# One stage in place of three in the third layer of a graph network kernel

## The chip, the cores and the metric

The kernel runs on one core of one Trainium2 chip. A core has five engines with instruction streams of their own: TensorE (PE, matrix products, with its weight loads shown as PEld), VectorE (DVE), ScalarE (ACT), GpSimd (POOL) and SyncE (SP), and 16 DMA engines that move data between the core's memory and HBM. Each engine runs its stream strictly in order and waits on semaphores that others raise. The metric is the device time of one execution in microseconds (us), the median of several executions.

## The reference

Four graph layers stand behind each other; the third is the one concerned. It runs four steps over 5000 nodes with a state `h` of 128 numbers each and 80000 edges of four types:

```python
etypes = jnp.argmax(edge_feat, axis=1)
h = node_feat
for _ in range(N_STEPS):                                   # 4
    trans = jnp.einsum('nd,tod->tno', h, W_edge) + b_edge[:, None, :]
    msg = trans[etypes, src]
    a = jax.ops.segment_sum(msg, dst, num_segments=N)
    h = _gru_cell(a, h, W_ih, W_hh, b_ih, b_hh)

# _gru_cell(x, h): gi = x @ W_ih.T + b_ih, gh = h @ W_hh.T + b_hh, each split in r, z, n parts
#   r = sigmoid(ir + hr); z = sigmoid(iz + hz); n = tanh(inn + r * hn)
#   return (1 - z) * n + z * h
```

## The kernel before

The nodes are padded to 5120, which makes ten chunks of 512 (`CHUNKS`, `CHUNK`). The state `hT` is kept turned, features on the 128 partitions and nodes along the free dimension. All numbers are 32-bit floats; PSUM has eight banks, each of 128 x 512.

The program is a row of blocks. Inside a block each engine has its own stream, and a block ends for all engines together (line 82 in the trace). Semaphores used by a block are cleared by SP in a later block; `clear_block` is an empty block for that, at the end of a loop body. Most dense stages use the helper `pairs`, which runs chunks two at a time (`V = 2`) in a hardware loop, so that chunk `c` uses buffers and banks `u = c % 2` and one chunk is worked on while the other is read out.

Each of the four steps of the third layer (the loop over `L2_STEPS`) runs four stages:

- `projected_rows` ("l2_rows"): DVE copies a chunk of `hT` to a staging tile `xs` (L775), PE multiplies its four groups of 128 nodes with the 128 x 512 matrix of all four edge types (L799), DVE adds the bias into `rows` (L781) and SP stores 1 MB per chunk in the table `table_typed` (L816). Both PSUM sides are double: banks `4 * u + k`.
- `sum_pass` ("l2_sums"): POOL gathers one row of the table for each edge (L857), DVE builds selection matrices (L961), PE adds the rows up in PSUM (L979), ACT copies each finished bank of sums to `t1` (L944). Nodes lie on partitions there.
- `from_rows` ("l2_messages"): DVE copies a chunk of `t1` to a staging tile (L1498), PE turns it with four transposes (L1567), DVE copies the turned chunk back to `t1` (L1541).
- `gru` ("l2_gru"): for each chunk PE makes six products of 512 columns into four banks (`4 * u` to `4 * u + 3`, L1633 to L1636), ACT bends two of them with a sigmoid (L1644, L1645), DVE applies the reset gate (L1656, L1659), ACT takes the tanh (L1649), DVE updates the state in three operations (L1663, L1665, L1667).

What sets the order on PE in `gru` is `pairs`: the products of both chunks of a pair stand behind each other, and they wait only for banks that were read out two chunks ago:

```python
def project(c, u, i):
    at_least(pe, g_gated, c + 1 - V)
    at_least(pe, g_read, c + 1 - V)
```

Of the kernel before, what the change touches and what calls it, by code (L numbers as in the profile page):

```python
# [67 lines left out]
def program(nc, io, out):  # L68
    ctx = ExitStack()
    with ctx:  # L70
        def sb(name, shape, dt=F32, where=ctx):
            return where.enter_context(nc.sbuf_tensor(name, shape, dt))

        def sems(*names):
            return [ctx.enter_context(nc.semaphore(n)) for n in names]
# [4 lines left out]
        @contextmanager  # L80
        def block(name, *used):
            with nc.Block(name) as b:  # L82
                cleared = [s for s in spent if s not in used]
                assert len(cleared) == len(spent), name
                spent.clear()

                @b.sync
                def _(sp):
                    for s in cleared:
                        sp.sem_clear(s)  # L90
                yield b
            spent.extend(used)

        def clear_block(name):
            with block(name):
                pass
# [4 lines left out]
        table_typed = nc.dram_tensor("table_typed", [NP, 4 * D], F32)  # L101
# [8 lines left out]
        ident = sb("ident", [P, P])  # L110
# [4 lines left out]
        wt = sb("wt", [P, NW, P])  # L115
# [11 lines left out]
        gate_bias = sb("gate_bias", [P, 2, 2])  # L127
# [5 lines left out]
        bedge_rows = sb("bedge_rows", [P, 4 * D])  # L133
# [26 lines left out]
        def wcol(name, k=0):  # L160
            return vec[:, VEC[name] + k:VEC[name] + k + 1]
# [4 lines left out]
        with ExitStack() as tmp:  # L166
# [395 lines left out]
        ROWS = LOOPS * GROUP * 16  # L562

        TILE_COUNTS = [len(range(r, TILE_REGIONS, REGIONS)) * GROUP * 16 for r in range(REGIONS)]
# [13 lines left out]
        V = 2  # L578
        def pairs(eng, *stages, ahead=None):


            turns_of = CHUNKS // V

            def run(i, parts):
                for stage in parts:
                    for u in range(V):
                        stage(i * V + u, u, i)

            def turn(i):
                if ahead is not None and not (isinstance(i, int) and i + 1 == turns_of):  # L590
                    run(i + 1, [ahead])
                run(i, stages)
            if ahead is not None:
                run(0, [ahead])
            turn(0)
            with eng.Fori(1, turns_of - (ahead is not None)) as i:
                turn(i)
            if ahead is not None:
                turn(turns_of - 1)
# [103 lines left out]
        r_stored = sems(*(f"rows_stored{u}" for u in range(V)))  # L703
# [917 lines left out]
        def gru(name, msg, h, w_ih, w_hh, gates, b_in, b_hn):  # L1621

            with ExitStack() as tmp:
                gate = sb(f"{name}_gate", [P, V, 2, CHUNK], F32, tmp)
                new = sb(f"{name}_new", [P, V, CHUNK], F32, tmp)
                with block(name, g_product, g_gated, g_reset, g_new, g_read, g_step) as b:
# [26 lines left out]
                    def _(dve):  # L1653
# [13 lines left out]
                            dve.tensor_tensor(h[:, cols(c)], new[:, u, :], gate[:, u, 0, :], ALU.add).then_inc(g_step, 1)  # L1667
                        pairs(dve, reset, update)

        b_stats, b_root, b_applied, b_scale, b_done = sems("bn_step", "bn_rooted", "bn_applied", "bn_product", "bn_done")  # L1670

        def batch_norm(name, src, gain, shift, dst=None, residual=None, weight=None, bias=None):
# [63 lines left out]
        def add_state(name, src):  # L1736
            with block(name, a_added) as b:
                @b.vector
                def _(dve):
                    dve.tensor_tensor(resT[:], resT[:], src[:], ALU.add).then_inc(a_added, 1)  # L1740
# [55 lines left out]
        def parts_of(w, first, count):  # L1796
            return [w[:, first + k, :] for k in range(count)]
# [27 lines left out]
        with block("l2_index", l_typed) as b:  # L1825
            @b.sync
            def _(sp):
# [3 lines left out]
                               (w3[:, 6:8, :], io["L3_gnn_W2"].rearrange("(k p) f -> p k f", p=P))):  # L1831
                    sp.dma_start(to, of).then_inc(l_typed, 16)
                sp.wait_ge(l_typed, 16 * 7)
        with nc.Fori(0, L2_STEPS) as it:
            projected_rows("l2_rows", hT, wt[:, WEDGE:WEDGE + 4, :].rearrange("p a b -> p (a b)"), 4 * D, table_typed, bias=bedge_rows[:])
            sum_pass("l2_sums", table_typed.ap().rearrange("n (t f) -> (n t) f", f=D),
                     [GAT_ITERS * ROWS + n + it * n for n in TILE_COUNTS], t1)
            from_rows("l2_messages", t1, rows_in=t1)
            gru("l2_gru", t1, hT, parts_of(wt, GGIH, 3), parts_of(wt, GGHH, 3), gate_bias[:, 1, :], wcol("2_b_ih", 2), wcol("2_b_hh", 2))
            clear_block("l2_end")  # L1840
        add_state("l2_residual", hT)


# [29 lines left out]
```

## Time and profile before

| | us |
|---|---|
| median of 3 runs | 12100.61 |
| lowest and highest | 12093.36, 12107.19 |
| the profiled execution | 12019.95 |
| its span, first to last instruction | 12018.1 |
| PE busy, share of the span | 6550.1 (55%) |
| POOL busy, share of the span | 6209.6 (52%) |
| DVE busy, share of the span | 4612.7 (38%) |
| ACT busy, share of the span | 2251.5 (19%) |

The busy shares are means over many stages with different limits, so they say little of one stage. The third layer's steps run from 6498 to 10673 us of the span. The profiled execution was 80.7 us shorter than the median of the unprofiled ones, of which 1.9 us lie around the span. TensorE's granted clock is shown as a share of 2.4 GHz: 1.00 is 2.4 GHz, 0.50 is 1.2 GHz, and a value between is a mean over a stretch that had both.

### The profile page before, as it was taken

Reading aid. Unit: us, or ns where it says so; the run is one execution under the profiler, and the core shown is the slowest. Engines: PE = TensorE matmul, PEld = TensorE weight load, DVE = VectorE, ACT = ScalarE, POOL = GpSimd, SP = SyncE. Lnnn points to the kernel's source line nnn. Section 1 sums busy time; section 2 is a strip of 40 time slices with the busy share of each in tenths; the row PEclk is TensorE's granted clock in tenths of the full one; section 3 lists DMA queues with packets and bytes.
Section 4 is the critical chain, followed back from the end, with each engine's and each line's share of the span. In section 5 each row is a group of like instructions: output and inputs, shape, how many; then the busy total and the mean of one; then the engine's idle time right before and its main releaser. Section 6 shows DMA issues by size and latency. Waiting matters only on the chain. (4 is left out here: it accounts for less than half of the span.)

```text
span 12018.1 us, 148393 instructions
## 1 busy us (share of the span) xinstructions
PE 6550.1 (55%) x36272; PEld 5479.0 (46%) x36273; DVE 4612.7 (38%) x10118; ACT 2251.5 (19%) x4313; POOL 6209.6 (52%) x6365
## 2 busy tenths in 40 slices
PE   3666786566786665884335334433533443365555
PEld 3555665555765555853323223233323322244443
DVE  4444754444754444752113112211311221135555
ACT  1222552222542222641000000000000000011111
POOL 2666423666414665504663665466366456625553
PEclk6777898777897777996667666666766666677777
DMA  2444322444313443401111111211111121112221
GB/s 75 128 127 127 103 64 69 128 127 125 106 42 88 129 128 105 125 22 42 46 45 61 46 46 36 68 45 46 60 45 45 34 71 46 46 43 77 78 77 55
DMA packets 698434, 894.29 MB, mean 74 GB/s; under 512 B 148417, under 2 KB 443211, under 8 KB 698130
## 3 DMA queue, kind: packets, MB, share of 16 engines
q0 software_dynamic: 198368, 429.61, 13.6%
q1 hardware_dynamic: 498474, 461.96, 12.4%
q8 instruction: 51, 0.84, 0.0%
q14 instruction: 125, 1.02, 0.0%
q10 hardware_dynamic: 1416, 0.86, 0.0%
HBM read 698.72 MB, written 193.14 MB: 74 GB/s over the span
## 5 line engine op out<-in xcount | busy, mean ns | idle before, releaser
L857 POOL DMA_INDIRECT states<-table_typed,tile_idx x2512 | 2415.9, 962 | 1777.8 <-issue 721.2
L840 POOL DMA_INDIRECT states<-table_x,src_idx x2016 | 1980.1, 982 | 1862.7 <-POOLq L82 742.8
L979 PE MATMUL psum<-states,l_sums_select 128*128 x4480 | 905.5, 336 | 1729.7 <-issue 1696.3
L979 PEld LDWEIGHTS psum<-states,l_sums_select 128*128 128x128 f32 x4480 | 777.0, 244 | 1854.3 <-issue 1853.8
L961 DVE SCALAR_TENSOR_TENSOR l_sums_select<-dst_all,pair_start,iota_row 128x512 f32<-128x512 f32 x560 | 402.1, 749 | 2212.5 <-remote 1401.0
L1091 PE MATMUL psum<-ident,select 128*128 128x128 f32 x2016 | 418.3, 344 | 1199.3 <-DVE states L1059 723.4
L840 POOL DMA_INDIRECT l_pass_ring<-table_kv,src_idx x672 | 655.1, 975 | 658.9 <-DVE score L1312 286.3
L1068 DVE TENSOR_TENSOR states<-w,psum 128x512 f32<-128x512 f32 x504 | 345.2, 685 | 1544.0 <-ACT w L1048 969.0
L857 POOL DMA_INDIRECT states<-table_x,tile_idx x628 | 602.1, 959 | 626.2 <-POOLq L82 337.0
L979 PE MATMUL psum<-states,select 128*128 x2240 | 469.4, 348 | 808.8 <-issue 769.4
L944 ACT COPY t<-psum 128x512 f32<-128x512 f32 x50 | 29.3, 585 | 4534.1 <-PE psum L979 2586.3
L1091 PEld LDWEIGHTS psum<-ident,select 128*128 128x128 f32 x2016 | 297.9, 178 | 1263.5 <-DVE states L1059 567.3
L979 PEld LDWEIGHTS psum<-states,select 128*128 128x128 f32 x2240 | 404.7, 254 | 876.7 <-issue 876.0
L1144 POOL TENSOR_TENSOR w<-iota_row,dst_local 128x512 f32<-128x512 f32 x504 | 524.3, 1041 | 459.7 <-ACT select L1161 459.7
L1108 PE MATMUL psum<-t,l_scores_spread 128*128 x4032 | 675.2, 317 | 72.1 <-issue 71.6
L1105 PE MATMUL psum<-wt,l_scores_mixT 128*128 128x128 f32 x4032 | 713.5, 336 | 0.0
L1105 PEld LDWEIGHTS psum<-wt,l_scores_mixT 128*128 128x128 f32 x4032 | 672.1, 252 | 0.6 <-issue 0.2
L1108 PEld LDWEIGHTS psum<-t,l_scores_spread 128*128 128x128 f32 x4032 | 630.4, 233 | 75.8 <-issue 75.7
L961 DVE SCALAR_TENSOR_TENSOR select<-dst_all,pair_start,iota_row 128x512 f32<-128x512 f32 x280 | 200.2, 749 | 1035.7 <-remote 567.1
L1231 PE MATMUL psum<-l_values_msg,select 128*128 128x132 f32 x4032 | 549.5, 279 | 68.2 <-DVE l_values_msg L1171 68.2
L1048 ACT COPY w<-psum 128x512 f32<-128x512 f32 x504 | 300.5, 596 | 1355.7 <-remote 844.0
L1220 PE MATMUL psum<-wt,l_values_ring 128*128 128x128 f32 x4032 | 535.7, 277 | 15.4 <-DMA l_values_ring<-rows_dram 15.4
(357 smaller groups left out, 11997.4 us busy)
## 6 DMA issues: line engine op xcount, KB each, us to landing
states<-in_edge_attr_dram SPq DMA_DIRECT2D x2016, 64.0 KB
rows_dram<-l_scores_mixT SPq DMA_DIRECT2D x504, 256.0 KB
l_values_ring<-rows_dram SPq DMA_DIRECT2D x504, 256.0 KB
table_typed<-l_rows_rows SPq DMA_DIRECT2D x40, 1024.0 KB, 4.3
states<-table_typed,tile_idx POOLq DMA_INDIRECT x2512
states<-table_x,src_idx POOLq DMA_INDIRECT x2016
l_pass_ring<-table_kv,src_idx POOLq DMA_INDIRECT x672
table_x<-l_rows_rows SPq DMA_DIRECT2D x40, 256.0 KB, 2.3
```

Of the source, the lines that this page charges most:

```text
L840: pool.indirect_dma_start(out=ring[:, k % REGIONS, u, :], out_offset=None, in_=table, in_offset=at).then_inc(gathered[k % REGIONS], 16)
L857: pool.indirect_dma_start(out=ring[:, k % TILE_RING, u, :], out_offset=None, in_=table, in_offset=at).then_inc(gathered[k % REGIONS], 16)
L961: dve.scalar_tensor_tensor(out=picked(k), in0=dst_all[:, bass.ds(column, GROUP)].unsqueeze(2).broadcast_to([P, GROUP, P]), scalar=pair_sta ...
L979: ins = pe.matmul(to, picked(k)[:, u, :], rows, start=False, stop=True, skip_group_check=True)
L1048: act.copy(key[:, r % 2, :, :], keys(r)).then_inc(p_evacuated, 1)
L1068: dve.tensor_tensor(prod.rearrange("p (a b) f -> p a b f", a=2), key[:, r % 2, :, :].rearrange("p (a b) f -> p a b f", a=2), queries(r)[:, ...
L1091: pe.transpose(psum[:, 0, u * P:(u + 1) * P], select[:, r, u, :], ident[:])
L1105: pe.matmul(keys(r)[:, u, :], mixT[:, r, u, :], wt[:, WK, :], start=True, stop=True)
L1108: ins = pe.matmul(queries(r)[:, u // pair, u % pair, :], spread[:, r % 2, u, :], q, start=True, stop=True)
L1144: pool.tensor_tensor(away[:, r % 2, :, :], iota_row[:].unsqueeze(1).broadcast_to([P, GROUP, P]), dst_local[:, bass.ds(step_of(i, r), GROUP ...
L1220: ins = pe.matmul(values(r)[:, u, :], ring[:, r, u, :], wt[:, WV, :], start=True, stop=True)
L1231: ins = pe.matmul(sums(r, u), select[:, r, u, :], msg[:, r, u, :], start=True, stop=True)
```

## The change

`from_rows`, `gru` and the next step's `projected_rows` become one block, `gated_update`, written out over ten chunks. Ahead of the loop stands one `projected_rows` and a `clear_block`; the loop runs three steps of `sum_pass` and `gated_update`; a fourth `sum_pass` and a `gated_update` without projection follow it. The transposes read `t1` in place and the projection reads `hT` in place; ACT copies the turned sums to `msgT`. The working tiles lie in `states`, which is free between two sum passes. The four gate banks are now banks 1 to 4 for every chunk, bank 0 holds the turned sums, and banks 5 to 7 go round for the projection.

`waves` runs the stages of different chunks in one order: at each turn `t`, projection of chunk `t - 2`, gates of chunk `t - 1`, turning of chunk `t`.

```diff
+        def gated_update(name, msg, h, w_ih, w_hh, gates, b_in, b_hn, rhs=None, bias=None, table=None):
...
+            def waves(*stages):
+                for t in range(CHUNKS + len(stages) - 1):
+                    for lag in reversed(range(len(stages))):
+                        if 0 <= t - lag < CHUNKS:
+                            stages[lag](t - lag)
...
+                    def turn(c):
+                        at_least(pe, u_copied, c)
+                        for k in range(4):
+                            ins = pe.transpose(psum[:, 0, k * P:(k + 1) * P], msg[:, c * CHUNK + k * P:c * CHUNK + (k + 1) * P], ident[:])
+                        ins.then_inc(u_turned, 1)
+                    def gates_of(c):
+                        at_least(pe, u_gated, c)
+                        at_least(pe, u_read, c)
+                        pe.matmul(psum[:, 4, :], w_hh[2], h[:, at(c)], start=True, stop=True)
+                        for k in range(2):
+                            pe.matmul(psum[:, 1 + k, :], w_hh[k], h[:, at(c)], start=True, stop=False)
+                        pe.wait_ge(u_copied, c + 1)
+                        for k in range(2):
+                            pe.matmul(psum[:, 1 + k, :], w_ih[k], msgT[:, c % V, :], start=False, stop=True)
+                        pe.matmul(psum[:, 3, :], w_ih[2], msgT[:, c % V, :], start=True, stop=True).then_inc(u_product, 1)
+                    def next_rows(c):
+                        pe.wait_ge(u_step, 3 * c + 3)
+                        for k in range(4):
+                            at_least(pe, u_kept, 4 * c + k - 2)
+                            pe.matmul(psum[:, 5 + (4 * c + k) % 3, :], h[:, c * CHUNK + k * P:c * CHUNK + (k + 1) * P], rhs,
+                                      start=True, stop=True).then_inc(u_projected, 1)
+                    waves(*([turn, gates_of, next_rows] if project else [turn, gates_of]))
...
+                    def copy(c):
+                        act.wait_ge(u_turned, c + 1)
+                        at_least(act, u_product, c + 1 - V)
+                        act.copy(msgT[:, c % V, :], psum[:, 0, :]).then_inc(u_copied, 1)
+                    def bend(c):
+                        act.wait_ge(u_product, c + 1)
+                        at_least(act, u_step, 3 * (c + 1 - V))
+                        act.activation(gate[:, c % V, 0, :], psum[:, 1, :], ACT.Sigmoid, bias=gates[:, 0:1])
+                        act.activation(gate[:, c % V, 1, :], psum[:, 2, :], ACT.Sigmoid, bias=gates[:, 1:2]).then_inc(u_gated, 1)
+                        act.wait_ge(u_read, c + 1)
+                        act.activation(new[:, c % V, :], new[:, c % V, :], ACT.Tanh, bias=b_in).then_inc(u_new, 1)
+                    waves(copy, bend)
...
+                    for t in range(CHUNKS + 1):
+                        if project and t >= 1:
+                            keep(t - 1, 0)
+                            keep(t - 1, 1)
+                        if t < CHUNKS:
+                            reset(t)
+                        if project and t >= 1:
+                            keep(t - 1, 2)
+                            keep(t - 1, 3)
+                        if t < CHUNKS:
+                            update(t)
...
+                            sp.dma_start(table[at(c), :].rearrange("(b p) f -> p b f", p=P), rows[:, c % V, :, :]).then_inc(r_stored[c % V], 16)
...
-        with nc.Fori(0, L2_STEPS) as it:
-            projected_rows("l2_rows", hT, wt[:, WEDGE:WEDGE + 4, :].rearrange("p a b -> p (a b)"), 4 * D, table_typed, bias=bedge_rows[:])
-            sum_pass("l2_sums", table_typed.ap().rearrange("n (t f) -> (n t) f", f=D),
-                     [GAT_ITERS * ROWS + n + it * n for n in TILE_COUNTS], t1)
-            from_rows("l2_messages", t1, rows_in=t1)
-            gru("l2_gru", t1, hT, parts_of(wt, GGIH, 3), parts_of(wt, GGHH, 3), gate_bias[:, 1, :], wcol("2_b_ih", 2), wcol("2_b_hh", 2))
...
+        projected_rows("l2_rows", hT, by_type, 4 * D, table_typed, bias=bedge_rows[:])
+        clear_block("l2_start")
+        with nc.Fori(0, L2_STEPS - 1) as it:
+            sum_pass("l2_sums", typed_rows, [GAT_ITERS * ROWS + n + it * n for n in TILE_COUNTS], t1)
+            gated_update("l2_update", t1, hT, *l2_gates, rhs=by_type, bias=bedge_rows[:], table=table_typed)
             clear_block("l2_end")
+        sum_pass("l2_last_sums", typed_rows, [GAT_ITERS * ROWS + L2_STEPS * n for n in TILE_COUNTS], t1)
+        gated_update("l2_last_update", t1, hT, *l2_gates)
```

`reset`, `update` and `keep` on DVE are the operations of L1656, L1659, L1663, L1665, L1667 and L781 of the kernel before, on the new tiles. In the changed kernel their lines are L1748, L1751 (reset), L1755, L1757, L1759 (update) and L1744 (keep); on PE L1700 is `turn`, L1706 to L1712 `gates_of`, L1718 `next_rows`.

In the kernel before, PE's stream at the start of the gated update holds the products of a pair of chunks (`t1` is the turned sums, `hT` the state, `wt` the weights):

```order
L1633 MATMUL psum<-t1,wt 128x512
L1634 MATMUL psum<-hT,wt 128x512
L1633 MATMUL psum<-t1,wt 128x512
L1634 MATMUL psum<-hT,wt 128x512
L1635 MATMUL psum<-t1,wt 128x512
L1636 MATMUL psum<-hT,wt 128x512
L1633 MATMUL psum<-t1,wt 128x512
```

In the changed kernel PE's stream from the start of the fused block reads (`states` is `msgT` there, and L1718 with `wt,hT` the projection of the chunk whose gates stand ahead of it):

```order
L1700 MATMUL psum<-ident,t1 128x128 x4
L1706 MATMUL psum<-hT,wt 128x512
L1708 MATMUL psum<-hT,wt 128x512 x2
L1711 MATMUL psum<-states,wt 128x512 x2
L1712 MATMUL psum<-states,wt 128x512
L1700 MATMUL psum<-ident,t1 128x128 x4
L1718 MATMUL psum<-wt,hT 128x512 x4
L1706 MATMUL psum<-hT,wt 128x512
L1708 MATMUL psum<-hT,wt 128x512 x2
L1711 MATMUL psum<-states,wt 128x512 x2
L1712 MATMUL psum<-states,wt 128x512
```

Between the gates of one chunk (first L1706 to L1712) and the gates of the next now stand four transposes and the projection of the first chunk.

DVE's stream of the kernel before, at the start of the gated update, holds two resets and then two updates:

```order
L1656 SCALAR_TENSOR_TENSOR l2_gru_new<-psum,vec,l2_gru_gate 128x512
L1659 TENSOR_TENSOR l2_gru_new<-l2_gru_new,psum 128x512
L1656 SCALAR_TENSOR_TENSOR l2_gru_new<-psum,vec,l2_gru_gate 128x512
L1659 TENSOR_TENSOR l2_gru_new<-l2_gru_new,psum 128x512
L1663 TENSOR_TENSOR l2_gru_gate<-hT,l2_gru_new 128x512
L1665 TENSOR_TENSOR l2_gru_gate<-l2_gru_gate 128x512
L1667 TENSOR_TENSOR hT<-l2_gru_new,l2_gru_gate 128x512
```

In the changed kernel it goes, from the update of the first chunk on (all working tiles are in `states`):

```order
L1755 TENSOR_TENSOR states<-hT,states 128x512
L1757 TENSOR_TENSOR states<-states 128x512
L1759 TENSOR_TENSOR hT<-states 128x512
L1744 TENSOR_TENSOR states<-psum,bedge_rows 128x512 x2
L1748 SCALAR_TENSOR_TENSOR states<-psum,vec,states 128x512
L1751 TENSOR_TENSOR states<-states,psum 128x512
L1744 TENSOR_TENSOR states<-psum,bedge_rows 128x512 x2
L1755 TENSOR_TENSOR states<-hT,states 128x512
```

Two of the four bias additions of one chunk now stand ahead of the next chunk's reset, and two between its reset and its update.

## Rows read from the trace of the kernel before

**Rows 1.** The page's first line: the span.

```profile
span 12018.1 us, 148393 instructions
```

**Rows 2.** Busy time by stage: sum pass, messages, gated update, table rows.

```profile
core 0: us, PE busy (x) PEld busy (x) DVE busy (x) ACT busy (x) POOL busy (x), PEclk, DMA share, GB/s
6551.00:7469.30 918.30, 329.65 (x1584) 277.04 (x1582) 139.81 (x196) 8.33 (x13) 604.70 (x628) 0.61 0.17 45
7469.30:7484.60 15.30, 8.97 (x40) 7.13 (x40) 10.31 (x20) 0.00 (x0) 0.00 (x0) 0.60 0.00 0
7484.60:7545.90 61.30, 53.90 (x120) 23.51 (x120) 34.01 (x51) 20.58 (x31) 0.00 (x0) 0.95 0.00 0
7545.90:7594.10 48.20, 37.18 (x80) 15.41 (x80) 27.99 (x51) 0.00 (x0) 0.00 (x0) 0.95 0.50 188
```

**Rows 3.** Timeline, stage borders: start, us, engine, line, operation, [idle before <-releaser].

```profile
7468.69 0.58 ACT L944 COPY t<-psum 128x512 f32<-128x512 f32 x1 [18.41 <-PE psum L979]
...
7547.18 0.17 DVE L788 MEMSET t<- 128x128 f32 x1 [1.32 <-PEq L82]
...
7591.58 2.48 DVE L781 TENSOR_TENSOR l_rows_rows<-psum,bedge_rows 128x512 f32<-128x512 f32 x4 [0.29 <-DMA table_typed<-l_rows_rows]
...
7599.71 0.94 POOL L857 DMA_INDIRECT states<-table_typed,tile_idx  x1 [155.02 <-POOLq L82]
...
10595.26 0.58 ACT L944 COPY t<-psum 128x512 f32<-128x512 f32 x1 [23.17 <-PE psum L979]
...
10671.76 0.69 DVE L1667 TENSOR_TENSOR hT<-l_gru_new,l_gru_gate 128x512 f32 x1
```

**Rows 4.** Timeline, the last pair of chunks of a gated update.

```profile
7537.83 1.02 PE L1636 MATMUL psum<-hT,wt 128*128 x2
7538.97 0.69 ACT L1644 ACTIVATE l_gru_gate<-psum,gate_bias 128x512 f32<-128x512 f32 x1 [3.88 <-PE psum L1636]
7539.56 0.68 ACT L1645 ACTIVATE l_gru_gate<-psum,gate_bias 128x512 f32<-128x512 f32 x1
...
7540.27 0.75 DVE L1656 SCALAR_TENSOR_TENSOR l_gru_new<-psum,vec,l_gru_gate 128x512 f32<-128x512 f32 x1 [3.33 <-ACT l_gru_gate L1645]
7541.06 0.69 DVE L1659 TENSOR_TENSOR l_gru_new<-l_gru_new,psum 128x512 f32<-128x512 f32 x1
...
7541.78 0.72 ACT L1649 ACTIVATE l_gru_new<-l_gru_new,vec 128x512 f32<-128x512 f32 x1 [0.93 <-DVE l_gru_new L1659]
...
7543.72 0.68 DVE L1663 TENSOR_TENSOR l_gru_gate<-hT,l_gru_new 128x512 f32<-128x512 f32 x1
...
7545.16 0.69 DVE L1667 TENSOR_TENSOR hT<-l_gru_new,l_gru_gate 128x512 f32 x1
```

**Rows 5.** Timeline, two chunks of the table rows.

```profile
7565.08 4.87 DVE L781 TENSOR_TENSOR l_rows_rows<-psum,bedge_rows 128x512 f32<-128x512 f32 x8
7565.82 7.13 PE L799 MATMUL psum<-wt,select 128*128 128x512 f32 x16 [1.25 <-DVE l_rows_rows L781]
```

**Rows 6.** Timeline of PE: first matmuls behind a wait (three from the score pass).

```profile
312.65 1.09 PE L1091 MATMUL psum<-ident,select 128*128 128x128 f32 x4 [4.99 <-ACT l_scores_mixT L1040]
...
818.99 0.66 PE L1091 MATMUL psum<-ident,select 128*128 128x128 f32 x4 [2.59 <-ACT l_scores_mixT L1040]
...
1115.08 0.66 PE L1091 MATMUL psum<-ident,select 128*128 128x128 f32 x4 [2.52 <-ACT l_scores_mixT L1040]
...
7547.68 8.64 PE L799 MATMUL psum<-wt,select 128*128 128x512 f32 x16 [8.82 <-DVE select L775]
```

**Rows 7.** Busy time and granted clock (PEclk) behind three of these waits.

```profile
312.60:317.60 5.00, 4.95 (x23) 4.99 (x24) 2.84 (x5) 1.47 (x3) 3.78 (x5) 0.50 0.53 151
...
818.80:821.00 2.20, 2.02 (x13) 2.02 (x14) 1.37 (x3) 1.11 (x4) 1.59 (x3) 0.70 0.34 115
821.00:826.00 5.00, 5.00 (x37) 4.99 (x36) 1.46 (x3) 0.59 (x2) 3.78 (x5) 0.79 0.59 173
...
7547.60:7550.70 3.10, 3.02 (x4) 1.48 (x5) 0.35 (x2) 0.00 (x0) 0.00 (x0) 0.50 0.03 8
```

More of the change, by code:

```diff
@@ L1668, in _, with at, keep, reset @@
                         pairs(dve, reset, update)
+        u_turned, u_copied, u_product, u_gated, u_reset, u_read, u_new, u_step, u_projected, u_kept = sems(
+            "sums_turned", "sums_copied", "gate_products", "gates_made", "reset_applied", "gate_banks_read", "new_made", "state_step",
+            "next_projected", "next_kept")
+        def gated_update(name, msg, h, w_ih, w_hh, gates, b_in, b_hn, rhs=None, bias=None, table=None):
+            room = states[:, 0:V * (4 + 4 * 4) * CHUNK // 2]
+            msgT = room[:, 0:V * CHUNK].rearrange("p (u f) -> p u f", u=V)
+            gate = room[:, V * CHUNK:3 * V * CHUNK].rearrange("p (u k f) -> p u k f", u=V, k=2)
+            new = room[:, 3 * V * CHUNK:4 * V * CHUNK].rearrange("p (u f) -> p u f", u=V)
+            rows = room[:, 4 * V * CHUNK:4 * V * CHUNK + V * 4 * CHUNK].rearrange("p (u k f) -> p u k f", u=V, k=4)
+            project = rhs is not None
+            def at(c):
+                return slice(c * CHUNK, (c + 1) * CHUNK)
+            def waves(*stages):
[3 more added lines that the diff above has]
+                            stages[lag](t - lag)
+            with block(name, u_turned, u_copied, u_product, u_gated, u_reset, u_read, u_new, u_step, u_projected, u_kept, *r_stored) as b:
+                @b.tensor
+                def _(pe):
+                    def turn(c):
[20 more added lines that the diff above has]
+                    waves(*([turn, gates_of, next_rows] if project else [turn, gates_of]))
+                @b.scalar
+                def _(act):
+                    def copy(c):
[10 more added lines that the diff above has]
+                    waves(copy, bend)
+                @b.vector
+                def _(dve):
+                    def keep(c, k):
+                        dve.wait_ge(u_projected, 4 * c + k + 1)
+                        if c >= V:
+                            dve.wait_ge(r_stored[c % V], c // V * 16)
+                        dve.tensor_tensor(rows[:, c % V, k, :], psum[:, 5 + (4 * c + k) % 3, :], bias, ALU.add).then_inc(u_kept, 1)
+                    def reset(c):
+                        dve.wait_ge(u_gated, c + 1)
+                        dve.scalar_tensor_tensor(out=new[:, c % V, :], in0=psum[:, 4, :], scalar=b_hn, in1=gate[:, c % V, 0, :],
+                                                 op0=ALU.add, op1=ALU.mult).then_inc(u_reset, 1)
+                        dve.wait_ge(u_reset, c + 1)
+                        dve.tensor_tensor(new[:, c % V, :], new[:, c % V, :], psum[:, 3, :], ALU.add).then_inc(u_read, 1)
+                    def update(c):
+                        dve.wait_ge(u_new, c + 1)
+                        dve.tensor_tensor(gate[:, c % V, 0, :], h[:, at(c)], new[:, c % V, :], ALU.subtract).then_inc(u_step, 1)
+                        dve.wait_ge(u_step, 3 * c + 1)
+                        dve.tensor_tensor(gate[:, c % V, 0, :], gate[:, c % V, 0, :], gate[:, c % V, 1, :], ALU.mult).then_inc(u_step, 1)
+                        dve.wait_ge(u_step, 3 * c + 2)
+                        dve.tensor_tensor(h[:, at(c)], new[:, c % V, :], gate[:, c % V, 0, :], ALU.add).then_inc(u_step, 1)
+                    for t in range(CHUNKS + 1):
[9 more added lines that the diff above has]
+                            update(t)
+                if project:
+                    @b.sync
+                    def _(sp):
+                        for c in range(CHUNKS):
+                            sp.wait_ge(u_kept, 4 * c + 4)
+                            sp.dma_start(table[at(c), :].rearrange("(b p) f -> p b f", p=P), rows[:, c % V, :, :]).then_inc(r_stored[c % V], 16)
+                        for stored in r_stored:
+                            sp.wait_ge(stored, 16 * (CHUNKS // V))
@@ L1833, in _ @@
                 sp.wait_ge(l_typed, 16 * 7)
-        with nc.Fori(0, L2_STEPS) as it:
-            projected_rows("l2_rows", hT, wt[:, WEDGE:WEDGE + 4, :].rearrange("p a b -> p (a b)"), 4 * D, table_typed, bias=bedge_rows[:])
-            sum_pass("l2_sums", table_typed.ap().rearrange("n (t f) -> (n t) f", f=D),
-                     [GAT_ITERS * ROWS + n + it * n for n in TILE_COUNTS], t1)
-            from_rows("l2_messages", t1, rows_in=t1)
-            gru("l2_gru", t1, hT, parts_of(wt, GGIH, 3), parts_of(wt, GGHH, 3), gate_bias[:, 1, :], wcol("2_b_ih", 2), wcol("2_b_hh", 2))
+        by_type = wt[:, WEDGE:WEDGE + 4, :].rearrange("p a b -> p (a b)")
+        typed_rows = table_typed.ap().rearrange("n (t f) -> (n t) f", f=D)
+        l2_gates = (parts_of(wt, GGIH, 3), parts_of(wt, GGHH, 3), gate_bias[:, 1, :], wcol("2_b_ih", 2), wcol("2_b_hh", 2))
+        projected_rows("l2_rows", hT, by_type, 4 * D, table_typed, bias=bedge_rows[:])
[3 more added lines that the diff above has]
+            gated_update("l2_update", t1, hT, *l2_gates, rhs=by_type, bias=bedge_rows[:], table=table_typed)
             clear_block("l2_end")
+        sum_pass("l2_last_sums", typed_rows, [GAT_ITERS * ROWS + L2_STEPS * n for n in TILE_COUNTS], t1)
+        gated_update("l2_last_update", t1, hT, *l2_gates)
         add_state("l2_residual", hT)
```

## The prediction

> **What bounds the kernel now.** I read the span first [rows 1], then cut one step of the third layer into its stages by busy time [rows 2]. The sum pass takes 918.3 us and is not touched; the change can only act on what stands between the end of one sum pass and the first gather of the next. The three stages there are 15.3, 61.3 and 48.2 us long. The reader should see which engine fills each: in the gated update PE is busy 53.9 of 61.3 us, in the table rows 37.2 of 48.2 us, and the granted clock is 0.95 in both, so PE's work at 2.4 GHz is the bound there, while in the messages stage it is a round between DVE and PE at a mean clock of 0.60. Third, I take the exact borders from the timeline [rows 3]: the last copy of sums ends at 7469.27 (7468.69 + 0.58), the last bias addition of the table rows at 7594.06, the first gather starts at 7599.71. From sums to the last bias addition are **124.8 us**, three times over. The last step has no table rows behind it: 10595.84 to 10672.45, **76.6 us**. The first table rows stay as they are.
>
> **PE's work per chunk.** A 32-bit product of 512 columns is two records. Eight of the projection's take 7.13 us [rows 5]; less about 0.2 us by which the last record outlasts its turn that is 0.86 us a product at full clock, and the gate products have the same length (L1636, 1.02 us with that overlap) [rows 4]. Six gate products make 5.14 us, four projections 3.43 us, together 8.57 us. Four transposes take 1.09 us at the low clock and 0.66 with overlap at the full one, some 0.43 us of pitch [rows 6]. So the fused stage asks PE for 9.0 us a chunk. None of this is saved. What goes are DVE's copies: L1498 and L1541, 20 operations in 10.3 us, with the messages stage of 15.3 us that they set [rows 2], and L775 in the table rows, where DVE is busy only 28.0 of 48.2 us, so that one costs little now.
>
> **What the change adds: a wait in PE's stream.** PE runs in order, and the order is gates of chunk c, turning of c+1, projection of c, gates of c+1. The projection waits for the finished state of chunk c, which needs the whole round trip through ACT and DVE; the gates of c+1, which need nothing of it, are queued behind that wait. Before, the gates of the next pair filled it. The length of the round trip, from rows 4: PE could start its next product at 7538.69 (7537.83 + 0.86). ACT's first sigmoid starts at 7538.97, the second ends at 7540.24, DVE's reset runs from 7540.27 and its second operation starts at 7541.06. Behind that, DVE now does two bias additions of the chunk before, 0.60 us apart each by (4.87 - 0.68) / 7 [rows 5], so the update can start at 7542.86; the tanh would be done at 7542.50, so the two additions, and not the tanh, come last, by 0.36 us. The update takes 2.13 us, from 7543.72 to 7545.85 in its row, so it ends at 7545.0, and PE starts 0.05 us later. That is **6.36 us** in which PE has 0.43 us of transposes. At full clock a chunk takes 8.57 + 6.36 = 14.93 us.
>
> ACT's new copy (0.58 us, as L944 [rows 3]) and the turning of the next chunk lie inside this wait; both are free as long as the wait is there. The table load that ACT does once at the sigmoid lies ahead of the first product. The stores (1 MB a chunk) have two chunks' time to land; before they made DVE wait only 0.29 us at the end [rows 3], where a chunk took 4.2 us. Behind the last bias addition the store and the block end take the same 5.6 us to the first gather as before.
>
> **The clock.** What does PE's clock do behind a wait of almost 6 us? Behind 4.99 us of waiting in the score pass it resumed at 1.2 GHz and stayed there for 5.0 us of work; behind 8.82 us, at the head of the table rows, for 3.1 us [rows 6, 7]. Half of such a stretch is lost: 2.5 and 1.55 us. I take 2.0 us a chunk, the middle, which gives **16.93 us**. The Trainium skill ("TensorE: Matmul & The Clock Gate", section "HAM oscillation — how this bites in real kernels") says that waits between bursts throttle PE again each time, so that every burst starts cold; rows 6 and 7 agree. By that rule alone the sum would be the same as with rows.
>
> **The sum, fused stage.** Block start 0.35 us, first chunk's turning and gates 7 us (5.6 at full clock, up to 1.5 more), nine further chunks 152.4 us, and at the end the round trip, projection at a partly low clock and last addition, 6.36 + 3.43 + 2.0 + 0.8 = 12.6 us: 172.3 us in place of 124.8. That is +47.5 us, three times: **+142.6**. Clear blocks: an empty block costs about 1 us (a border with one took 1.32 us in row L788 [rows 3], one without about 0.35); before one lay inside each 124.8 us, now it lies behind each fused stage and one ahead of the loop: +3 net.
>
> **The last update** has no projection, but its gate banks are no longer double: gates of c+1 wait until DVE has read chunk c's banks, 7541.75 + 0.05 less 7538.69, 3.11 us [rows 4]. At full clock a chunk takes 8.25 us, where two chunks of the gated update before took 61.3 / 5 = 12.3 us, 6.1 each. PE waits 2.7 us of it. Behind 2.59 us the clock fell just after PE had resumed (granted 0.70, then 0.79 over 7.2 us, 3.4 us at 1.2 GHz, 1.7 lost), behind 2.52 us the four transposes ran at the full rate, as their 0.66 us show [rows 6, 7]. Our wait is longer than both; I take 1.45 us a chunk, 9.7 us. 0.35 + 7 + 87.3 + 6.0 for the last round trip = 100.7 us in place of 76.6: **+24.1**. The Trainium skill ("Perfetto Trace Analysis", section "Matmuls") advises to let matmul groups go round through PSUM banks so that reading out one overlaps the next; the gate banks now do the opposite, and the trace agrees: with two sets a chunk took 6.1 us.
>
> All together 142.6 + 3 + 24.1 = **+170 us**. The profiled execution took 12019.95 us and would take 12190; against the median, 80.7 us higher, 12100.6 + 170 = **12270**.
>
> **The rivals.**
> - *The clock stays at 2.4 GHz.* Against it, rows 6 and 7; for it, only that 2.52 us did nothing. Fused stage 0.35 + 5.8 + 134.4 + 10.6 = 151.1, last 0.35 + 5.8 + 74.3 + 6 = 86.4: 79 + 3 + 10 = +92, 12192 us.
> - *The clock never rises.* A chunk takes 17.14 + 6.36 = 23.5 us, the fused stage 237, the last 138: +400, 12501 us. Against it: both long waits were followed by a rise after 3 to 5 us of work, and PE has 9 here.
> - *Faster: PE is not held up*, because the wait for the state is shorter than I read, or covered. It decides where the round trip falls under the 0.43 us of transposes. Then PE's 9.0 us a chunk is the period: 0.35 + 5.8 + 81 + 10.6 = 97.8 us, and 62 in the last: -81 + 3 - 14 = -92, 12008 us. The profile speaks against it: ACT's two sigmoids and DVE's five operations stand one behind the other in rows 4. The Trainium skill ("Perfetto Trace Analysis", section "Optimization Strategy") says that interleaving stages with different limits may help; that would be this case, and no row here supports it, since both long stages have the same limit, PE.
>
> **How the numbers follow.** Chances: forecast 0.84, full clock 0.08, low clock 0.03, faster 0.04, no change 0.01. Bounds of the forecast: low stretches of 3.1 to 5.0 us over some 30 bursts, -13 to +15; four stage starts, -6 to +6; the last update without a fall or with 1.7 us each, -13 to +2; code written out over ten chunks that has to be fetched, 0 to +15; spread of runs 7. That is about 12225 to 12315; I give 12225 to 12320. About 0.2% (24 us) is what a measurement of this kernel can tell from no change. Faster 0.04, same 0.01, slower 0.95.
>
> **What would show it.** In the changed profile, PE should wait about 5.9 us in each chunk of the fused stage ahead of L1718, released by DVE's L1759, with a granted clock well under 0.95 there; a chunk should take 16 to 18 us, and the sums should be 172 us ahead of the last bias addition. In the last update PE waits some 2.7 us for L1751. Sum passes stay at 918 us; if they move, the forecast is wrong for a reason that I haven't seen. It falls if PE waits for something else, or if L1744 holds up the update by more than 0.4 us.

## The result and the profile after

| | median us | lowest, highest | runs |
|---|---|---|---|
| before | 12097.06 | 12093.36, 12107.19 | 4 |
| changed | 12278.91 | 12258.27, 12288.55 | 4 |

The ratio is 1.0146 (95% interval 1.013 to 1.0162): slower by 182 us, where 170 had been forecast. The time lies in the range.

The busy time by stage of the changed kernel reads as follows: a sum pass, the three fused stages, and the last update. The columns are those of [rows 2].

```profile
6615.10:7538.50 923.40, 342.71 (x1584) 287.84 (x1582) 139.52 (x196) 8.35 (x13) 604.73 (x628) 0.60 0.17 45
7538.50:7712.20 173.70, 115.75 (x240) 50.50 (x240) 60.32 (x90) 26.00 (x41) 0.00 (x0) 0.80 0.14 55
8645.60:8818.10 172.50, 114.52 (x240) 50.10 (x240) 60.31 (x90) 26.02 (x42) 0.00 (x0) 0.80 0.14 55
9754.80:9927.40 172.60, 114.67 (x240) 50.14 (x240) 60.31 (x90) 26.01 (x42) 0.00 (x0) 0.80 0.14 55
10862.10:10964.00 101.90, 73.20 (x160) 32.26 (x160) 35.13 (x50) 24.72 (x40) 0.00 (x0) 0.84 0.00 0
```

The fused stage takes 172.9 us in the mean where the three stages of [rows 2] took 124.8, and the last update 101.9 in place of 76.6. PE is busy for only two thirds of the fused stage, at a mean granted clock of 0.80, where it was busy for 53.9 of 61.3 us at 0.95 in the gated update before.

One chunk of the second fused stage, with PE, ACT and DVE in order of time:

```profile
8770.27 1.02 PE L1712 MATMUL psum<-states,wt 128*128 128x512 f32 x2
8771.13 0.60 PE L1700 MATMUL psum<-ident,t 128*128 128x128 f32 x4
8771.33 0.69 ACT L1732 ACTIVATE states<-psum,gate_bias 128x512 f32<-128x512 f32 x1 [13.07 <-PE psum L1712]
8771.92 0.68 ACT L1733 ACTIVATE states<-psum,gate_bias 128x512 f32<-128x512 f32 x1
8772.63 0.75 DVE L1748 SCALAR_TENSOR_TENSOR states<-psum,vec,states 128x512 f32<-128x512 f32 x1 [7.78 <-ACT states L1733]
8773.42 0.69 DVE L1751 TENSOR_TENSOR states<-states,psum 128x512 f32<-128x512 f32 x1
8774.02 1.28 DVE L1744 TENSOR_TENSOR states<-psum,bedge_rows 128x512 f32<-128x512 f32 x2
8774.14 0.72 ACT L1735 ACTIVATE states<-states,vec 128x512 f32<-128x512 f32 x1 [1.54 <-DVE states L1751]
8774.77 0.57 ACT L1727 COPY states<-psum 128x512 f32<-128x512 f32 x1
8775.22 0.68 DVE L1755 TENSOR_TENSOR states<-hT,states 128x512 f32<-128x512 f32 x1
...
8776.66 0.69 DVE L1759 TENSOR_TENSOR hT<-states 128x512 f32<-128x512 f32 x1
8777.41 2.07 PE L1718 MATMUL psum<-wt,hT 128*128 128x512 f32 x2 [5.68 <-DVE hT L1759]
```

This is the round trip of [rows 4] with nothing of PE's own behind it: the gates end (L1712), PE turns the next chunk (L1700), and then waits 5.68 us for the state (L1759), although the gates of the next chunk could start from 8774.1 on, when L1751 has read their banks. The two bias additions L1744 stand between reset and update. From 8771.13, when PE could go on, to 8777.41 are 6.28 us; 6.36 had been forecast. (The trace counts the wait from the end of the last transpose, 0.60 us behind the start of the first; the forecast took 0.43 us for them and so named 5.9 us.) The projection resumes at 1.2 GHz: two records take 2.07 us where L1636 took 1.02 at the full clock [rows 4].

The starts of the projection in the same stage, the first two, then three from further on:

```profile
8657.51 6.02 PE L1718 MATMUL psum<-wt,hT 128*128 128x512 f32 x8 [5.36 <-DVE hT L1759]
...
8674.79 5.91 PE L1718 MATMUL psum<-wt,hT 128*128 128x512 f32 x8 [5.68 <-DVE hT L1759]
...
8743.27 5.81 PE L1718 MATMUL psum<-wt,hT 128*128 128x512 f32 x8 [5.68 <-DVE hT L1759]
...
8760.34 5.80 PE L1718 MATMUL psum<-wt,hT 128*128 128x512 f32 x8 [5.68 <-DVE hT L1759]
...
8777.41 5.80 PE L1718 MATMUL psum<-wt,hT 128*128 128x512 f32 x8 [5.68 <-DVE hT L1759]
```

The distance is 17.28 us at first, falls from chunk to chunk and stays at 17.07; in the first fused stage it begins at 17.90 and ends at 17.07 too. 16.93 had been forecast.

In the last update PE waits for L1751, which frees its gate banks:

```profile
10911.01 1.48 PE L1706 MATMUL psum<-hT,wt 128*128 128x512 f32 x2 [2.52 <-DVE states L1751]
10912.29 3.23 PE L1708 MATMUL psum<-hT,wt 128*128 128x512 f32 x4
10915.36 1.88 PE L1711 MATMUL psum<-states,wt 128*128 128x512 f32 x4
...
10921.06 1.28 PE L1706 MATMUL psum<-hT,wt 128*128 128x512 f32 x2 [2.52 <-DVE states L1751]
```

A chunk takes 10.05 us. The clock falls just behind the wait (here within L1706, 1.48 and 1.28 us where it takes 1.02 at the full clock) and rises again within the chunk: L1708, four records as L1711, takes 3.23 us, and L1711 1.88 at the full clock.

**The sum by stages.** 3 x (172.9 - 124.8) = 144.3 and 101.9 - 76.6 = 25.3. The rest is at the borders. These are the last bias addition and the first gather behind each fused stage:

```profile
7711.47 0.69 DVE L1744 TENSOR_TENSOR states<-psum,bedge_rows 128x512 f32<-128x512 f32 x1 [0.17 <-PE psum L1718]
...
7721.86 0.95 POOL L857 DMA_INDIRECT states<-table_typed,tile_idx  x1 [207.19 <-issue]
...
8817.38 0.69 DVE L1744 TENSOR_TENSOR states<-psum,bedge_rows 128x512 f32<-128x512 f32 x1 [0.17 <-PE psum L1718]
...
8827.23 0.94 POOL L857 DMA_INDIRECT states<-table_typed,tile_idx  x1 [204.74 <-issue]
...
9926.72 0.69 DVE L1744 TENSOR_TENSOR states<-psum,bedge_rows 128x512 f32<-128x512 f32 x1 [0.17 <-PE psum L1718]
...
9934.03 0.95 POOL L857 DMA_INDIRECT states<-table_typed,tile_idx  x1 [206.53 <-POOLq L82]
```

The borders are 9.7, 9.2 and 6.6 us long where the kernel before had 5.6 [rows 3]: +8.6 in sum, where 3 had been forecast, a clear block of about 1 us in each. Together 178 us, against 182 between the medians.

The two profiled executions are further apart, 268.6 us (spans of 12286.7 and 12018.1). Of the 90 us beyond the 178, 64 lie ahead of the third layer's first gather and 49 in its four sum passes, while the part behind the last update was 23 us shorter. None of this is work that the change touches, and the kernel before, profiled once more beside the experiments, had a span of 12083.5 us and longer sum passes too (below).

### The profile page after: what moved, and what is told of

Its sections match the earlier page's. It is cut to its first block and busy times, and to the rows that moved or that the text cites. A ratio compares the mean times of both kernels' runs of the same rounds, so it can differ in the third digit from the quotient of the medians.

```text
span 12286.7 us, 147339 instructions
## 1 busy us (share of the span) xinstructions
PE 6656.5 (54%) x36272; PEld 5548.1 (45%) x36273; DVE 4567.5 (37%) x10005; ACT 2264.9 (18%) x4351; POOL 6218.4 (51%) x6365
## 5 line engine op out<-in xcount | busy, mean ns | idle before, releaser
L979 PE MATMUL psum<-states,l_sums_select 128*128 x3584 | 729.5, 339 | 1394.3 <-issue 1347.8
L979 PEld LDWEIGHTS psum<-states,l_sums_select 128*128 128x128 f32 x3584 | 628.1, 246 | 1487.3 <-issue 1486.7
L961 DVE SCALAR_TENSOR_TENSOR l_sums_select<-dst_all,pair_start,iota_row 128x512 f32<-128x512 f32 x448 | 322.4, 750 | 1784.7 <-remote 1240.7
L979 PE MATMUL psum<-states,select 128*128 x2240 | 494.1, 360 | 791.7 <-issue 737.0
```

What stands on the lines that cost most here:

```text
L961: dve.scalar_tensor_tensor(out=picked(k), in0=dst_all[:, bass.ds(column, GROUP)].unsqueeze(2).broadcast_to([P, GROUP, P]), scalar=pair_sta ...
L979: ins = pe.matmul(to, picked(k)[:, u, :], rows, start=False, stop=True, skip_group_check=True)
```

## The experiments

The first four ran in one series, where the kernel before had a median of 12077.21 us (12058.96 to 12097.15, 13 runs); the last three in a later one, where it took 10645.89 us (10640.44 to 10649.58, 7 runs). The reason for this difference is not shown. In the traces of the later series each sum pass of the third layer takes 803 to 805 us, where those of the earlier one show 915 to 926; that is some 450 of the 1431 us, and the rest lies ahead of and behind the third layer. So ratios are to the kernel before in the same series, and stages are compared by their own length.

### Gates ahead of the projection

```diff
-                    waves(*([turn, gates_of, next_rows] if project else [turn, gates_of]))
+                    for t in range(CHUNKS + 2):
+                        if 0 <= t - 1 < CHUNKS:
+                            gates_of(t - 1)
+                        if project and t >= 2:
+                            next_rows(t - 2)
+                        if t < CHUNKS:
+                            turn(t)
```

> The changed kernel with one thing moved on PE: the gates of chunk c+1 are issued ahead of the projection of chunk c, so that the wait for the finished state lies behind 5.1 us of gate products. All else is as in the changed kernel. Theory (the wait of the projection, with the next gates queued behind it, is the cost): PE no longer waits 5.7 us a chunk and its clock stays at 1.00; a chunk takes 9.0 to 9.3 us in place of 17.1 (PE's 9.0 us of work, perhaps 0.2 us because DVE's reset now stands behind two bias additions that come later), each fused stage 98 to 101 us in place of 172.9, the whole about 12060 us, 220 us under the changed kernel and some 35 under the kernel before. The last update has no projection and stays at 102 us. Rival (the cost lies in the single set of gate banks or in the tiles read in place): the fused stage stays above 150 us.

Measured: 12039.1 us, ratio to before 0.9974 (0.9962 to 0.9985). Here are the second fused stage, its beginning up to the first projection, and two starts of its projection:

```profile
8544.30:8646.80 102.50, 94.39 (x240) 42.63 (x240) 59.43 (x90) 25.99 (x42) 0.00 (x0) 0.98 0.24 92
8544.30:8558.60 14.30, 11.46 (x33) 5.50 (x34) 3.52 (x5) 4.33 (x7) 0.00 (x0) 1.00 0.00 0
```

```profile
8558.58 3.60 PE L1718 MATMUL psum<-wt,hT 128*128 128x512 f32 x8
...
8567.94 3.60 PE L1718 MATMUL psum<-wt,hT 128*128 128x512 f32 x8
```

From the first of these starts on the wait is gone, the clock of the stage is 0.98, a chunk takes 9.36 us in place of 17.07, and the stage 102.5 (102.6 and 104.3 in the other two) in place of 172.9. With the same work, the same single gate banks and the same tiles, one exchange of order on PE makes the change faster than the kernel before. So the cost was the wait of the projection and what was queued behind it. The stage was 1.5 to 3 us above the expected 98 to 101: the last projection still waits for its state (3.69 us) and runs in part at the low clock. The last update, which this edit doesn't touch, took 98.8 us and not 102, as it did in the run below: behind the first of its waits the clock didn't fall. So some 3 us of the gain aren't the exchange's.

### Work put into the wait

```diff
                     def next_rows(c):
+                        at_least(pe, u_kept, 4 * c - 2)
+                        for _ in range(5):
+                            pe.matmul(psum[:, 5 + (4 * c) % 3, :], w_hh[0], msgT[:, c % V, :], start=True, stop=True)
                         pe.wait_ge(u_step, 3 * c + 3)
```

> The changed kernel with work added: five idle products of 512 columns (0.86 us each at full clock) ahead of the projection's wait, into the PSUM bank that the projection overwrites next; their results are used by nothing. The round trip through ACT and DVE is untouched. Theory (6.3 us of round trip, and on top a clock that falls in it): the clock stays at 1.00, a chunk takes 14.9 to 15.2 us in place of 17.1, each fused stage 150 to 153 us in place of 172.9, the whole about 12215 us, some 62 under the changed kernel although PE does 4.3 us more a chunk. Rival (the clock costs nothing, the 17.1 us are all round trip): no change, 17.1 us a chunk, or more.

Measured: 12191.68 us, ratio 1.0094 (1.0078 to 1.0111). The first fused stage, and PE in one chunk of the second:

```profile
7526.70:7677.70 151.00, 136.00 (x340) 60.00 (x340) 60.26 (x90) 26.05 (x42) 0.00 (x0) 1.00 0.17 63
```

```profile
8670.59 0.60 PE L1700 MATMUL psum<-ident,t 128*128 128x128 f32 x4
8671.03 4.46 PE L1717 MATMUL psum<-states,wt 128*128 128x512 f32 x10
8676.86 3.70 PE L1721 MATMUL psum<-wt,hT 128*128 128x512 f32 x8 [1.38 <-DVE hT L1762]
```

With 4.3 us of idle products a chunk the stage is 22 us shorter: the clock stays at 1.00, the projection takes 3.70 us in place of 5.80, and a chunk 14.96. So of the 48.1 us that a fused stage lost, 22 are the clock and 26 the round trip itself. The Trainium skill ("TensorE: Matmul & The Clock Gate", section "HAM oscillation — how this bites in real kernels") says that waits between bursts make each burst start cold; this run agrees, by 2.1 us a chunk. The round trip itself was the same, 6.27 us from the transposes to the projection.

### The last update as before

```diff
-        gated_update("l2_last_update", t1, hT, *l2_gates)
+        from_rows("l2_messages", t1, rows_in=t1)
+        gru("l2_gru", t1, hT, *l2_gates)
```

> The changed kernel with one part undone: the last step's turning and gated update are the two stages of the kernel before, with double gate banks. Theory: from the last copy of sums to the last state operation 76.6 us in place of 101.9, the whole 25 us less, about 12254 us; the three fused stages stay at 172.9 us. Rival (the last update costs nothing extra and its 101.9 us come from the state of the clock on entry): more than 90 us.

Measured: 12217.02 us, ratio 1.0124 (1.0107 to 1.0141), where the changed kernel has 1.0146. The last step:

```profile
10815.60:10890.30 74.70, 60.96 (x160) 29.04 (x160) 44.19 (x70) 19.30 (x30) 0.00 (x0) 0.92 0.00 0
```

It takes 74.7 us in place of 101.9; 76.6 had been expected, and the kernel before, profiled once more, took 75.7. The two old stages, copies and all, are 27 us shorter than the joined one with a single set of gate banks.

### The kernel before once more

> The kernel before once more, for its trace on the same chip as the other runs. The changed kernel's sum passes took 923 to 930 us, those of the kernel before 911 to 918 us, and the sum pass of the second layer, which the change doesn't touch, took 12 us more too. If this is a difference between executions, this run's sum passes can be as long as the changed kernel's; if the change does it, they are 911 to 918 us again.

Two of its sum passes:

```profile
6607.10:7527.30 920.20, 351.41 (x1584) 293.98 (x1582) 140.04 (x196) 8.32 (x13) 602.87 (x628) 0.60 0.16 45
7656.80:8579.80 923.00, 339.73 (x1584) 287.38 (x1582) 139.74 (x196) 8.32 (x13) 604.08 (x628) 0.61 0.16 45
```

The other two took 915.5 and 925.4, all four 3684 us, where the first profile of before had 3653 and the changed kernel 3703. The three runs above, which all keep the fused block between the sum passes, had 3670, 3684 and 3676, none of them more than this one. So longer sum passes don't come with the change. The third layer's first gather starts at 6607.1 here, in the changed kernel at 6615.1, in the first profile of before at 6551.0. So most of the 90 us by which the two first profiles differ beyond the 178 is a difference between executions of the same code.

### All bias additions ahead of the reset

```diff
+                        if project and t >= 1:
+                            keep(t - 1, 2)
+                            keep(t - 1, 3)
                         if t < CHUNKS:
                             reset(t)
-                        if project and t >= 1:
-                            keep(t - 1, 2)
-                            keep(t - 1, 3)
```

> The changed kernel with all four bias additions of a chunk ahead of the next chunk's reset on DVE, so that none stands between reset and update. That takes 0.6 us off the round trip (PE waits 5.36 us instead of 5.68 already in the first chunk, where no addition is in the way). Plain sum: a chunk takes 0.3 to 0.4 us less, 16.7 us, three fused stages 10 us less. What the changed kernel's trace suggests instead: the distance from chunk to chunk falls from 17.5 to exactly 17.07 us and stays there, so the clock's turns hold the period, and the chunk stays at 17.07 us with a shorter wait and a longer stretch at 1.2 GHz; the stages stay at 172 to 174 us.

Measured: 10824.63 us, ratio 1.0167 (1.015 to 1.0184). Starts of the projection in the second fused stage:

```profile
7807.94 6.12 PE L1718 MATMUL psum<-wt,hT 128*128 128x512 f32 x8 [5.36 <-DVE hT L1759]
...
7825.01 6.12 PE L1718 MATMUL psum<-wt,hT 128*128 128x512 f32 x8 [5.36 <-DVE hT L1759]
...
7842.07 6.12 PE L1718 MATMUL psum<-wt,hT 128*128 128x512 f32 x8 [5.36 <-DVE hT L1759]
```

The wait is 0.32 us shorter than in the changed kernel, the projection 0.32 us longer (6.12 us in place of 5.80), and the distance is 17.07 us as before. In the first stage the distance begins at 16.51 us, below that of the changed kernel, and grows to 17.07. The stages take 172.9, 172.3 and 173.6 us. The round trip was shortened by 0.32 us and nothing was gained: PE resumed earlier, but its clock rose no earlier. The plain sum was wrong here, and the reading by the clock right.

### The faster version

On top of the gates' new order, DVE does one bias addition ahead of the reset and three behind it; in the last update the gate banks are `4 * (c % 2)` to `4 * (c % 2) + 3`, the turned sums go through the third of them ahead of the product that is written there, and ACT copies them between sigmoids and tanh:

```diff
+            def gate_banks(c):
+                return (1, 2, 3, 4) if project else tuple(4 * (c % 2) + k for k in range(4))
+            def turned_in(c):
+                return 0 if project else gate_banks(c)[2]
...
-                        at_least(pe, u_gated, c)
-                        at_least(pe, u_read, c)
+                        at_least(pe, u_gated, c if project else c - 1)
+                        at_least(pe, u_read, c if project else c - 1)
...
-                    waves(copy, bend)
+                    for t in range(CHUNKS + 1):
+                        if t >= 1:
+                            bend(t - 1)
+                        if t < CHUNKS:
+                            copy(t)
+                        if t >= 1:
+                            renew(t - 1)
```

> The version with the gates of the next chunk ahead of the projection on PE, and two more edits: DVE does one bias addition ahead of the reset and three behind it (in the run with PE's order alone two stood ahead and the reset started 2.4 us after the gates' end), and the last update has two sets of four gate banks, with the turned sums in the bank of the fourth product, and ACT's copy ahead of its tanh. Theory (PE's own work is then the period): 9.0 to 9.1 us a chunk in the fused stage, 98 to 101 us; in the last update 5.6 us a chunk and 62 to 65 us in place of 99 to 102. The whole 40 to 50 us under the run with PE's order alone, 80 to 90 under the kernel before (ratio 0.993). Rival (something else in the last update, such as the clock, holds it): above 76 us there.

Measured: 10567.99 us, ratio 0.993 (0.9913 to 0.9947): the fastest version, 78 us under the kernel before. The second fused stage, its beginning up to the first projection, and the last update:

```profile
7613.70:7717.30 103.60, 96.56 (x240) 44.16 (x240) 59.36 (x90) 26.10 (x42) 0.00 (x0) 0.94 0.24 91
7613.70:7632.10 18.40, 15.54 (x33) 7.23 (x34) 3.51 (x5) 4.36 (x7) 0.00 (x0) 0.77 0.00 0
9444.80:9508.60 63.80, 57.71 (x160) 27.47 (x160) 35.13 (x50) 24.73 (x41) 0.00 (x0) 0.95 0.00 1
```

The last update takes 63.8 us, as expected: two sets of gate banks and a copy that comes in time make PE's 5.6 us a chunk the period. That is the Trainium skill's advice ("Perfetto Trace Analysis", section "Matmuls") to let matmul groups go round through PSUM banks; 100.7 us with one set, in the two other runs of this series, and 63.8 with two agree, though ACT's order was changed with it. In the fused stage the expectation missed. A chunk takes 9.02 us in place of 9.36, but the stage is no shorter than with the order alone, 103.6 to 104.3 us. What takes the gain back shows at its beginning, here in the second stage; the second line is its last projection:

```profile
7625.17 1.51 PE L1715 MATMUL psum<-hT,wt 128*128 128x512 f32 x2 [2.52 <-DVE states L1774]
...
7711.30 5.26 PE L1727 MATMUL psum<-wt,hT 128*128 128x512 f32 x8 [3.44 <-DVE hT L1782]
```

The second chunk's gates have no projection in front and wait 2.52 us for their banks, and the last projection waits 3.44 us. Both waits were there in the run with the order alone too (2.52 and 3.69 us). What differs is the clock: there the beginning ran at 1.00 in two of the three stages and the first projection started 14.3 us into the stage; here it has 0.77, and the first projection starts after 18.4 us (17.7 in the other two). From there to the end the stage takes 85 to 87 us, where it took 88.2 to 88.3. The sum passes of this series end at a granted clock of 0.50 to 0.54, those of the earlier one at 0.67 to 0.78, and of the six fused stages of the two other runs here five begin low as well. So the additions' order gains 2 to 3 us a stage, and a lower clock on entry, which this edit doesn't touch, hides it.

### The loop written out

```diff
-        with nc.Fori(0, L2_STEPS - 1) as it:
+        for it in range(L2_STEPS - 1):
```

> The changed kernel with its outer loop over three steps written out, so that no engine jumps back; the work is the same. In the changed kernel the first gather starts 9.7 and 9.2 us behind the last bias addition where the loop jumps back, and 6.6 us where it doesn't, and four instruction packets are fetched in the first of these gaps and none in the last. Theory (the code of the sum pass is fetched anew behind the jump and POOL waits for it): 6.6 us in all three places, 5 to 6 us less in the whole, which only the trace can show. Rival (it is the work of clearing semaphores or the store): 9 to 10 us in the first two places again.

Measured: 10818.2 us, ratio 1.0163 (1.0146 to 1.018), which can't be told by its time from 1.0167, the ratio of the run with the additions first. Two of its borders:

```profile
6868.95 0.69 DVE L1744 TENSOR_TENSOR states<-psum,bedge_rows 128x512 f32<-128x512 f32 x1 [0.17 <-PE psum L1718]
...
6876.44 0.94 POOL L857 DMA_INDIRECT states<-table_typed,tile_idx  x1 [188.92 <-POOLq L82]
...
7855.40 0.69 DVE L1744 TENSOR_TENSOR states<-psum,bedge_rows 128x512 f32<-128x512 f32 x1 [0.17 <-PE psum L1718]
...
7862.41 0.94 POOL L857 DMA_INDIRECT states<-table_typed,tile_idx  x1 [189.80 <-POOLq L82]
```

They are 6.8, 6.3 and (not shown) 6.3 us long, where the loop had 9.7, 9.2 and 6.6. So the jump back costs about 3 us each of the two times that it is taken, and the rival (semaphores or the store) is out. The queues of the changed kernel in its first border (7712 to 7722 us) had packets of instructions:

```profile
q14 instruction: 3, 0.02, 0.8%
q8 instruction: 1, 0.02, 0.6%
```

In its second border there were two, in its third, where the loop ends, none; with the loop written out there was one in the first border and none in the others. The Trainium skill ("Runtime: NRT & Kernel Launch", section "Instruction fetch mechanics") says that a taken branch to code outside the present pages forces a fetch before execution can go on; the packets agree, with POOL's gather 3 us later. That POOL waited for just these packets isn't shown directly. Before, the same jump led into the table rows, where POOL had nothing to do for 48 us.

## Why the prediction was right, point by point

- **The bound before.** PE's work in the two long stages, and a round between DVE and PE in the short one: nothing in the runs speaks against it. In the faster version PE's work is the period again, 9.02 us a chunk.
- **PE's work per chunk, 9.0 us.** Measured with the wait gone: 9.02 us.
- **The round trip, 6.36 us**, with DVE's two bias additions last and not the tanh: 6.28 us, and 0.32 us less without the additions, where 0.36 had been read.
- **The clock.** 2.0 us lost a chunk by the middle of two rows; measured 2.2 (the projection takes 5.80 us in place of 3.60). The forecast of 16.93 us a chunk against 17.07 was close, in part by luck: 2.0 was the middle between two rows of other stages, and it was treated as a price that adds to the round trip. It isn't: a round trip 0.32 us shorter was paid back to the full by a longer stretch at the low clock.
- **The fused stage.** 172.3 forecast, 172.9 measured. Two terms were off and cancelled: the first chunk's turning and gates took 5.6 us, at the full clock, and not 7, and the nine chunks behind it took, in the second stage, 153.7 us and not 152.4.
- **The last update.** 100.7 forecast, 101.9 measured; a chunk 10.05 us in place of 9.7, so the clock cost 1.8 us a chunk where 1.45 had been put, again offset by the first chunk's 5.6 us in place of 7. The wait shows as 2.52 us and not 2.7 only by the way in which it is counted: from the gates' end to the resumption are 3.12 us (3.11 forecast). Counted so, it is exactly as long as the wait that had left the clock alone in [rows 6], and not longer, as the prediction said; yet the clock fell here in each chunk. In the run with the gates first it did not fall behind the first wait of the last update, also of 2.52 us. So the length of a wait alone doesn't tell.
- **The borders** are the term that was mis-sized: +3 forecast, +8.6 measured. The clear blocks had been counted, but not that the jump back now stands directly ahead of the gathers. "Code written out over ten chunks that has to be fetched" had been put at 0 to 15 us; instruction packets were there, but with the jump back.
- **The sum passes** should stay at 918 us or the forecast be wrong for an unseen reason. In the changed kernel's profile they took 923 to 928. The reason is a difference between executions: the kernel before, profiled again, had 916 to 925.
- **The rivals.** The clock at 2.4 GHz throughout would give a chunk of 14.93 us; the run with the filled wait made that case and took 14.96. The faster rival, PE not held up, was made by the exchange of order. The prediction named a wait "shorter, or covered", but tied the case to a round trip of under 0.43 us. It needs no such thing: the round trip stayed, and gate products that don't depend on it covered it.

## What to carry to other kernels

When stages are joined into one in-order stream, look at what is queued behind each wait: an instruction that waits for a long round trip must have independent work in front of it, not behind it. Here the order of two calls decided between 102.5 to 104.3 us (gates of the next chunk ahead of the projection) and 172.9 us a stage, where the three stages apart took 124.8. And a buffer set that is halved to make room for the joining has to be looked at in every place that uses it, above all where the work that hid the single set is missing, as in the last step.

## What the runs showed of the hardware

- A period with a wait of more than 5 us in it settled at 17.07 us a chunk, from distances of 17.90 and of 16.51 us alike, and taking 0.32 us from its wait changed nothing: the stretch at 1.2 GHz grew by as much as the wait shrank. A gain of that size on such a path doesn't show.
- Idle products that nobody reads made a stage 22 us shorter (172.9 to 151.0), with a granted clock of 1.00 and the same round trip (6.27 and 6.28 us).
- A wait of 2.52 us was followed by the full clock in some places (the first two fused stages with the gates first) and by 1.2 GHz in others (each chunk of the changed kernel's last update).
- A jump back of the outer loop cost about 3 us, on POOL's gather; a border without it took 6.3 to 6.8 us, with it 9.2 to 9.7.
- The same kernel took 12077 us in one series and 10646 in a later one, with sum passes of about 920 us in the traces of the one and 805 in those of the other, while the fused stage of the changed kernel's code took 171 to 175 us in both.
